# A transformer layer on one core: attention outputs turned by DMA instead of TensorE, and the projection's LayerNorm folded into the residual sum

## The reference, cut to what matters

```python
x = x + _layernorm(attn(_layernorm(x)), eps=1e-5)      # over the last axis, no gain, no shift
x = x + _layernorm(ffn(_layernorm(x)), eps=1e-5)
# attn: qkv = x @ w_attn + b_attn; 16 heads of 32; rope by head index; causal softmax, times E**-0.5;
#       o @ w_proj + b_proj
# ffn:  h = gelu(bitlinear(x, w_fc)); bitlinear(h, w_proj)
# bitlinear(x, w): layer_norm(x, eps=1e-6), absmax-quantised, times ternarised w
```

## Time and profile before

| | |
|---|---|
| median of 3 runs | 1260.82 us (1259.26 to 1261.31) |
| the profiled execution's own time | 1258.53 us |
| its span in the trace | 1256.8 us |
| TensorE busy | 1156.8 us, 92% |
| VectorE busy | 972.4 us, 77% |
| ScalarE busy | 770.1 us, 61% |
| GpSimd busy | 592.8 us, 47% |
| mean granted TensorE clock | 0.977 of full speed |

### The profile page before, as it was taken

How to read it: one execution, slowest core, us unless ns; L and a number is a source line. 1 busy time by engine, 2 the same in 40 slices (tenths; PEclk the granted TensorE clock), 3 DMA queues, 4 the chain that set the end, 5 groups by cost and what they waited for, 6 DMA issues and landing times.

```text
span 1256.8 us, 24649 instructions
## 1 busy us (share of the span) xinstructions
PE 1156.8 (92%) x9204; PEld 634.7 (51%) x9204; DVE 972.4 (77%) x2862; ACT 770.1 (61%) x1430; POOL 592.8 (47%) x658
## 2 busy tenths in 40 slices
PE   6968799999999999999999999999999999987997
PEld 4434444555445554555445554555545554554443
DVE  5988778688787878779796888779786887868634
ACT  5568747675566646675476655766466755577480
POOL 2143216941398125961279314971369412981260
PEclk9978899999999999999999999999999999997999
DMA  9441220123111230121310231112301221001000
GB/s 347 106 159 38 73 59 9 27 60 95 49 36 27 66 112 4 33 60 35 109 25 17 68 89 43 35 33 62 110 5 31 61 80 30 3 2 45 16 9 34
DMA packets 75514, 72.37 MB, mean 58 GB/s; under 512 B 34721, under 2 KB 60289, under 8 KB 74243
## 3 DMA queue, kind: packets, MB, share of 16 engines
q1 hardware_dynamic: 75395, 70.79, 20.1%
HBM read 29.63 MB, written 8.39 MB: 30 GB/s over the span
## 4 chain that ended last, share of the span: by engine, by line
PE 51%; DVE 30%; ACT 11%; issue 3%; POOL 3%; DMA 2%; SPq 1%; POOLq 0%; ACTq 0%; DVEq 0%
PE gen L511 17%; PE down L559 16%; DVE score L1229 8%; PE pv L626 5%; DVE hT L1106 4%; PE score L587 4%; DVE probs L1106 2%; PE gen L578 2%; ACT probs L918 1%; POOL rstd L1620 1%; DVE qkn L1336 1%; DVE bn L1260 1%; DVE mx L1229 1%; DMA x2T<-b_proj 1%; DVE gen L1229 1%
## 5 line engine op out<-in xcount | busy, mean ns | idle before, releaser
L1620 POOL TENSOR_TENSOR rstd<-veps,mhalf 128x1 f32<-128x1 f32 (+1 forms) x104 | 67.0, 644 | 460.5 <-DVE veps L1309 312.4
L918 ACT ACTIVATE probs<-score 128x512 f16<-128x512 f32 x360 | 189.8, 527 | 102.4 <-PE score L602 102.4
L511 PE MATMUL gen<-x2T,t1T 128*128 128x512 f16 x1024 | 240.1, 379 | 3.3 <-ACT x2T L838 1.8
L1106 DVE TENSOR_TENSOR probs<-score,probs 128x512 f16<-128x512 f32 x360 | 199.5, 595 | 45.1 <-ACT score L920 44.0
L559 PE MATMUL down<-t2T,hT 128*128 128x512 f16 x960 | 221.1, 382 | 0.0
L920 ACT ACTIVATE score<-score 128x512 f32<-128x512 f32 x360 | 192.5, 535 | 0.0
L511 PE MATMUL gen<-xT,wa 128*128 128x512 f16 x672 | 156.0, 382 | 4.2 <-DVE mx L1229 3.7
L1106 DVE TENSOR_TENSOR hT<-gen,hT 128x512 f16<-128x512 f32 x156 | 105.8, 685 | 68.6 <-ACT gen L866 34.5
L511 PEld LDWEIGHTS gen<-x2T,t1T 128*128 128x128 f16 x1024 | 95.5, 97 | 107.3 <-ACT x2T L838 4.5
L1229 DVE CUSTOM_DVE_ANT_0 score<-score,mask_rows 128x512 f32<-128x512 f32 (+3 forms) x312 | 143.0, 520 | 0.0
L559 PEld LDWEIGHTS down<-t2T,hT 128*128 128x128 f16 x960 | 90.3, 98 | 98.5 <-issue 2.7
(11 more groups left out here) (190 smaller groups left out, 1822.7 us busy)
## 6 DMA issues: line engine op xcount, KB each, us to landing
qk<-qkn SPq DMA_DIRECT2D x360, 64.0 KB, 2.0
xo<-x SPq DMA_DIRECT2D x8, 1024.0 KB, 5.7
out<-xn SPq DMA_DIRECT2D x31, 256.0 KB, 2.2
hT<-x SPq DMA_DIRECT2D x7, 1024.0 KB, 6.3
hT<-w_fc SPq DMA_DIRECT2D x4, 1024.0 KB, 16.2
hT<-w_down SPq DMA_DIRECT2D x4, 1024.0 KB, 5.2
t2T<-w_qk SPq DMA_DIRECT2D x4, 512.0 KB, 7.4
probs<-w_v SPq DMA_DIRECT2D x1, 1024.0 KB, 10.3
```

The costliest lines, as they stand in the source:

```text
L511: mm = nc.tensor.matmul(bank[:, :], a, b, start=(start and n == 0), stop=(stop and n == len(pairs) - 1))
L918: nc.scalar.activation(probs[:, h % 2, HI, 512 * i:512 * i + n], bank[:, 0:n], ACT.Exp, scale=1.0 / S_UP)
L1106: return V.tensor_tensor(out, whole, hi, ALU.subtract)
```

## The change

The attention outputs of four heads (a chunk of 128 features, `o_chunk[c]`) are split into fp16 halves when the four heads are done, after heads 4, 8 and 12 (`OUT_AT`) and after head 15: `outputs_high` on ScalarE, `outputs_low` on VectorE. SP turns each half with a DMA transpose (`turn_outputs`) straight into the place of `x2T`, one after each `stack(g)`; the last chunk's stand between the first two and the last two heads of `stack(3)`. The fp32 transposes on TensorE and their evictions go. `project` is cut by chunks: `project(0)` and `project(1)` for chunks 0 to 2, then `values(1)`, then the rest. `load_x` waits for the DMA transposes instead of for `o_turn(3)`.

`normalise_y` goes. `first_sum` multiplies the projection's rows in PSUM by `rstd` and adds x in one scalar_tensor_tensor; the row's constant is left out there, where the next LayerNorm takes it away again, and GpSimd adds it to the final LayerNorm's `shift` (`late_shift` keeps one that would be overwritten). `v_low(1)` moves ahead of `y_moments(0)`, `values(1)` on ScalarE ahead of `normalise2(0)`.

```diff
+OUT_AT = {4: 0, 8: 1, 12: 2}
...
-        for name, n in (("v", 0), ("oT", 0), ("oT", 1), ("oT", 2), ("oT", 3), ("v", 1), ("x2T", 0), ("v", 2), ("x2T", 1), ("v", 3),
-                        ("x2T", 2), ("x2T", 3)):
+        for name, n in (("v", 0), ("v", 1), ("x2T", 0), ("v", 2), ("x2T", 1), ("v", 3), ("x2T", 2), ("x2T", 3)):
...
+        oT = x2T
+        o_more = o_more_sb[:, :]
+        o_chunk = [xo[:, c, :].rearrange("p (b e) -> p b e", b=TB) for c in range(EC)]
+        o_rows = [(o_more if c == 0 else xo[:, c - 1, :]).bitcast(f16).rearrange("p (a n) -> p a n", a=2) for c in range(EC)]
...
                     if b != 1:
-                        sp.wait_ge(g_full, g0 - AFTER_O)
+                        for c in range(EC):
+                            sp.wait_ge(oT_in[c], 32 * j)
...
+                def turn_outputs(c):
+
+                    for half in (HI, LO):
+                        sp.wait_ge((o_hi, o_lo)[half], EC * j + c + 1)
+                        sp.dma_start_transpose(oT[:, half, c, :].rearrange("p (b t) -> p b t", b=TB), o_rows[c][:, half, :]
+                                               ).then_inc(oT_in[c], 16)
+
...
@@ -435,7 +448,11 @@
                         row = TB * j if isinstance(j, int) else sp.snap(TB * j)
                         sp.dma_start(xres, x_v[:, bass.ds(row, TB), :]).then_inc(xres_in, 16)
                     if nxt:
-                        stack(g)
+                        stack(g, range(2) if g == 3 and here else range(4))
+                    if here:
+                        turn_outputs(g)
+                    if nxt and g == 3 and here:
+                        stack(g, range(2, 4))
                     if prev:
                         for tb in ((), (0, 1), (2,), (3,))[g]:
                             store(tb)
...
-
-                    if tb == 0:
-                        pe.wait_ge(o_scaled, len(SCALED))
-                        pe.wait_ge(o_ready, HEADS * (j + 1) - len(SCALED))
-                    bank = claim("oT", tb)
-                    turn(bank, lambda c: xo[:, tb, PARTS * c:PARTS * (c + 1)]).then_inc(g_full, 1)
-
-                def project(tb):
-
-                    if setup and tb == 0:
-                        pe.wait_ge(w_ready, 2)
-                    if tb < 3:
-                        pe.wait_ge(s_drained, s0 + S["scores", HEADS - 1 if nxt else HEADS - 2] + tb + 1)
-                    else:
-                        pe.wait_ge(pv_drained, HEADS * (j + 1))
+                def project(tb, c0, c1):
+
                     bank = y_banks[tb]
-                    products(bank, [(lift[:, :], p_bias[:, :])], stop=False)
-                    pe.wait_ge(oT_hi, TB * j + tb + 1)
-                    products(bank, [(oT[:, tb % 2, HI, c, :], wp[:, b, c, :]) for c in range(EC) for b in (HI, LO)],
-                             start=False, stop=False)
-                    drained("oT", tb)
-                    products(bank, [(oT[:, tb % 2, LO, c, :], wp[:, HI, c, :]) for c in range(EC)], start=False
-                             ).then_inc(y_full, 1)
+                    if c0 == 0:
+                        if setup and tb == 0:
+                            pe.wait_ge(w_ready, 2)
+                        if tb < 3:
+                            pe.wait_ge(s_drained, s0 + S["scores", HEADS - 1 if nxt else HEADS - 2] + tb + 1)
+                        else:
+                            pe.wait_ge(pv_drained, HEADS * (j + 1))
+                        products(bank, [(lift[:, :], p_bias[:, :])], stop=False)
+                    rows = slice(PARTS * tb, PARTS * (tb + 1))
+                    for c in range(c0, c1):
+                        pe.wait_ge(oT_in[c], 32 * (j + 1))
+                        last_one = products(bank, [(oT[:, HI, c, rows], wp[:, HI, c, :]), (oT[:, HI, c, rows], wp[:, LO, c, :]),
+                                                   (oT[:, LO, c, rows], wp[:, HI, c, :])], start=False, stop=(c == EC - 1))
+                    if c1 == EC:
+                        last_one.then_inc(y_full, 1)
 
                 def x2_turn(tb):
...
                 if here:
-                    o_turn(0)
-                    o_turn(1)
-                    project(0)
-                    o_turn(2)
-                    project(1)
-                    o_turn(3)
-                    project(2)
-                    project(3)
+                    project(0, 0, EC - 1)
+                    project(1, 0, EC - 1)
+                    if nxt:
+                        values(1)
+                    project(0, EC - 1, EC)
+                    project(1, EC - 1, EC)
+                    project(2, 0, EC)
+                    project(3, 0, EC)
                     if setup:
                         pe.wait_ge(tern_ready, 2 * FC)
                         for u in range(FC):
                             mm = nc.tensor.matmul(down[:, :], ones16[:, :], t2T[:, u, :], start=(u == 0),
                                                   stop=(u == FC - 1))
                         mm.then_inc(c_full, 1)
-                    if nxt:
-                        values(1)
...
-                    nc.scalar.activation(y_sb[:, tb % 2, :], y_banks[tb][:, :], ACT.Identity,
-                                         bias=shift[:, LP, tb:tb + 1], scale=rstd[:, LP, tb:tb + 1]
-                                         ).then_inc(y_ready, 1)
+                def outputs_high(c):
+
+                    done = 4 * (c + 1)
+                    need(act, o_scaled, len([h for h in SCALED if h < done or not setup]))
+                    act.wait_ge(o_ready, HEADS * j + done - len([h for h in SCALED if h < done or not setup]))
+                    need(act, o_lo, EC * j + c)
+                    high(o_rows[c][:, HI, :], o_chunk[c].rearrange("p b e -> p (b e)")).then_inc(o_hi, 1)
 
                 def normalise2(tb):
                     if tb < 2 and prev:
...
+                    if here and h in OUT_AT:
+                        outputs_high(OUT_AT[h])
...
                         final(FINISH_AT[h])
                 if here:
+                    outputs_high(EC - 1)
                     if nxt:
                         values(0)
-                    o_turned(0)
-                    o_turned(1)
-                    o_turned(2)
                     if prev and nxt:
                         final(3)
-                    normalise_y(0)
-                    o_turned(3)
-                    normalise_y(1)
-                    normalise2(0)
-                    normalise_y(2)
-                    normalise2(1)
-                    normalise_y(3)
                     if nxt:
                         values(1)
+                    normalise2(0)
+                    normalise2(1)
                     x2_turned(0)
                     if nxt:
                         values(2)
...
-                    V.tensor_tensor(xo[:, :, HD * h:HD * (h + 1)], oA[:, h % 2, :, :],
+                    V.tensor_tensor(o_chunk[h // 4][:, :, HD * (h % 4):HD * (h % 4 + 1)], oA[:, h % 2, :, :],
                                     r_sum[:, h % 2, :].unsqueeze(2).to_broadcast([PARTS, TB, HD]), ALU.mult
...
-                    low(oT[:, tb % 2, LO, :, :], blocks(bank_of("oT", tb)), oT[:, tb % 2, HI, :, :]
-                        ).then_inc(g_drained, 1)
+                def outputs_low(c):
+
+                    dve.wait_ge(o_hi, EC * j + c + 1)
+                    low(o_rows[c][:, LO, :], o_chunk[c].rearrange("p b e -> p (b e)"), o_rows[c][:, HI, :]).then_inc(o_lo, 1)
 
                 def y_moments(tb):
 
...
-                    dve.wait_ge(y_ready, n + 1)
-                    V.tensor_tensor(x1_out[:, tb, :], y_sb[:, tb % 2, :], xres[:, tb, :], ALU.add).then_inc(x1_ready, 1)
+                    dve.wait_ge(ln_ready[LP], n + 1)
+
+
+                    V.scalar_tensor_tensor(out=x1_out[:, tb, :], in0=y_banks[tb][:, :], scalar=rstd[:, LP, tb:tb + 1],
+                                           in1=xres[:, tb, :], op0=ALU.mult, op1=ALU.add).then_inc(x1_ready, 1)
...
                         head_output(h)
+                        if h in OUT_AT:
+                            outputs_low(OUT_AT[h])
...
                 if here:
+                    outputs_low(EC - 1)
                     if nxt:
                         v_low(0)
-                    o_low(0)
-                    o_low(1)
                     if prev and nxt:
                         final(3)
                         final_moments(3)
                         final_terms(3)
+                    if nxt:
+                        v_low(1)
                     y_moments(0)
-                    o_low(2)
                     y_moments(1)
-                    o_low(3)
                     first_sum(0)
                     y_moments(2)
                     first_sum(1)
                     y_moments(3)
                     first_sum(2)
-                    if nxt:
-                        v_low(1)
                     x2_low(0)
                     first_sum(3)
...
```

(20 more changed lines are left out.)

28 lines of the change are left out of this document (8 added, 20 removed).

## The result

| | before | after |
|---|---|---|
| median | 1260.89 us (1259.26 to 1261.31) | 1243.53 us (1239.58 to 1248.29) |
| after / before | | 0.9865, 95% interval 0.9833 to 0.9897 |
| profiled execution, its span | 1258.53, 1256.8 us | 1239.58, 1237.9 us |
| TensorE, VectorE busy | 1156.8, 972.4 us | 1139.9, 968.9 us |
| ScalarE, GpSimd busy | 770.1, 592.8 us | 746.7, 595.9 us |

A forecast was written before the change was run, and what follows sets the result against it. The usual tail was taken as bound by VectorE's LayerNorm chain, close to TensorE. Six usual batches 12.0, set-up 2.8, last batch 2.4, less 0.3 at the end, give 16.9 us saved: 1243.9 us, range 1239 to 1252.5.

The forecast's parts named there:

- 2.0 us a usual batch: Tail of each of six usual batches: VectorE's last small operation starts at 477.3 instead of 479.28, 12.0 us in all.
- the end's 0.3: At the kernel's very end, GpSimd's added small operation in the final LayerNorm is paid once, 0.27 us.
- rival C: Usual tail: TensorE is the bound, the sums cost no more; 2.5 us a batch, 1241 us; chance 0.15.
- `v_low(1)` leaving the chain with its wait (1.37): VectorE's usual tail: v_low(1) and its wait on ScalarE leave the chain, 0.6 + 0.77 us saved.
- a first sum 0.8 earlier: VectorE's usual tail: first_sum(0) starts at 466.8 instead of 467.62, 0.8 us earlier.
- 0.24 for dearer sums: VectorE's usual tail: the four first sums, now reading PSUM with a factor, cost 0.24 us more together.
- Part 2: Normalisation moved into first_sum: each sum with moments 1.91 us for 1.85, four times; GpSimd's addition 0.27 us.
- Covered: Head loop: subtractions at heads 4, 8, 12 cost nothing, hidden by VectorE's waits; 1.8 us a batch if uncovered.
- the 2.8 that this batch was to bring: Set-up batch's tail: VectorE waits there, so TensorE's whole saving counts, 2.8 us.
- The 0.6: Last batch with heads, before the tail: VectorE is the bound, so the subtraction at head 12 costs 0.6 us.
- A: Head loop gives the gain back: VectorE passes 1.8 us a batch to TensorE, 1256.5; chance 0.15 from 1249 up.
- B: Tail: last chunk's DMA transposes land late, about 10 us slower, 1271; chance 0.07 slower, 0.05 about break-even.

The follow-up runs named there:

- repeat: The changed kernel run once more with nothing edited; 1242.85 us, ratio 0.9871 to the kernel before.
- negm_once: Changed kernel with the four per-block negated means of y taken out of VectorE's chain, one for all behind first_sum(3); 1239.99 us, ratio 0.9852.
- more_products: Changed kernel with eight more TensorE products in the tail, four each in project(2) and project(3); 1249.05 us, ratio 0.9916.
- turn_only: Changed kernel with normalise_y kept on ScalarE: outputs turned by DMA, values(1) and v_low(1) still moved forward; 1252.26 us, ratio 0.9941.
- fold_only: Kernel before with only the normalisation folded into first_sum and GpSimd's extra addition, outputs still turned by TensorE; 1248.76 us, ratio 0.9919.
- best: Changed kernel, set-up chunks handled at heads 7, 9, 12, one negated mean for all blocks, values(1) back behind project(3) in usual batches; 1236.37 us, again 1238.13.
- late_chunk: Changed kernel with the last chunk's two transposes behind all twelve DMAs of stack(3) instead of behind six; 1249.02 us, ratio 0.9918.
- values_late: Changed kernel with values(1) back behind project(3), its eviction and v_low(1) also back in their old places; 1243.27 us, ratio 0.9867.
- best_2: As best, with the set-up batch's first three chunks handled at heads 10, 11 and 13, transposes behind stack(2); 1235.61 us, ratio 0.9806.

## Why the prediction was right, and where it was not

- The number and the size per batch. 2.0 us a usual batch was 2.07, the end's 0.3 was 0.32, the head loop of a usual batch cost nothing, the landings took 2.5 us in the median (2.4 to 4.1) and were hidden. In the usual tail the steps came where they were forecast, counted from `weigh(15)`'s start: moments at 9.0 us (9.0), the first sum at 11.3 (11.25), the last small operation at 21.8 (21.7). The last operation of the chain was forecast 19.9 us after `weigh(15)`'s end in the last batch and came 1165.71 - 1145.8 = 19.9 after it. That the median of after lies 0.4 us from the forecast is in part luck: its four times span 8.7 us, and between spans the saving was 18.9 us with the first profile and 14.6 with that of repeat, for 16.9 forecast. In the first profile two misses cancel, +2.2 in the set-up heads and 2.35 less than forecast in the loop of the last batch.
- VectorE's chain as the bound, against rival C. Right in the usual batches by negm_once and more_products; the set-up tail is TensorE's, also as forecast, 3.24 for 2.8.
- Which part earns it. The sum was made of `v_low(1)` leaving the chain with its wait (1.37) and a first sum 0.8 earlier, less 0.24 for dearer sums. As places in VectorE's queue the three held: the wait and `v_low(1)` are gone, the first sum starts 0.86 earlier (12.11 to 11.25 us after `weigh(15)`), each sum costs 0.06 more. Which edit brings them was taken wrongly. The wait of 0.77 goes by the fold alone, since ScalarE has four steps less; `v_low(1)` moved forward with values(1) ahead of the last chunk's products holds the chain's start back by 1.9 us, more than it saves, and hides 0.76 of what the turning gives. Part 2 was costed only by its dearer sum; that ScalarE's step between power and sum stood in the chain (1.2 us at the first sum) was not in it as a saving, and my expectations of turn_only and fold_only repeated that mistake after the result.
- The set-up batch. "Covered" was read from waits of a usual batch and taken for all. Its VectorE was not read in the set-up heads. A wait of 1.57 us more at head 4 is uncovered there, more than half of the 2.8 that this batch was to bring. That GpSimd can hold such a subtraction was in the text, with the price of 0.9 from the division; it took 0.84 more, at the place where no slot was free. The rest of the 2.0 to 4.5 us by which the set-up heads are longer in the kernels with the early chunk stays open: the clock dips there in every kernel, at other heads in each, and no run separates these dips from the change.
- The last batch. The tail was right (3.0 for 3.25). The loop gained 1.75 instead of losing 0.6, in a stretch that took 96.4 to 101.1 us across the kernels of the table; and 96.37 or 100.62 for one and the same kernel (best); so that gain says nothing about the change. In the two first profiles the same 825 instructions keep TensorE busy for 85.39 us at a granted clock of 0.93 before and for 82.28 at 0.96 after, more than the whole 1.75. The 0.6 is neither confirmed nor refuted.
- Rivals A and B. A did not happen in the usual batches and has its point in the set-up one. B is a matter of 1.8 us of slack (2.1 forecast), as late_chunk showed, and did not decide in after. C did not happen as told: the sums did cost 0.24 more, and TensorE is not the bound of a usual batch in after; it is near: behind the landing its waits add up to 0.7 us in values_late (0.43 and 0.26) and to 0.26 in best. The Trainium skill's price for a 128x128 transpose through DMA ("VectorE: DVE Perf Modes", "The three transpose paths") does not describe this: each half of a chunk, four blocks, lands in 2.5 us, and with 1309 ns a block (an estimate from that page's figure: eight blocks from 454.23 on, 464.7) TensorE would have waited in after at 459.31, which it does not.

## What to carry to other kernels

A step on another engine in the middle of a chain costs its hand-over where the chain has no other work to do meanwhile, here at the first of four sums. So a fold that makes the consumer dearer by 0.06 us was worth more (1.69 us a batch) than taking 2.8 us of work and waiting off another engine (1.14 on top of it); price it by the start of the first dependent instruction, not by its own duration. "It is hidden" has to be read in each kind of batch, set-up too. When a change is cut into halves to see which earns, a third edit that rides in one of them has to be cut out too. A piece of work used as cover for a transfer should not be longer than the transfer needs: here it hid the DMA and held back the chain.

## What the hardware showed

VectorE's 16-bit in-place pass over 128x512 in SBUF took 293 ns at heads 8 and 12, and 1134 to 1247 ns at head 4 while GpSimd worked on SBUF. The subtraction with two SBUF inputs took 1.52 us in the set-up batch, where it started inside a product of GpSimd, and 0.68 in the set-up batch of best_2, where it comes after GpSimd's last product. In the usual batches of after it meets GpSimd too, and there GpSimd pays. In all six the two start within 0.01 us of each other, and GpSimd's sum L1654 takes 1.80 us instead of 1.26 (in before none of these sums takes more than 1.28):

```profile
402.50 0.68 DVE L1104 TENSOR_TENSOR o_more<-xo,o_more 128x512 f16<-128x512 f32 x1
402.51 1.80 POOL L1654 TENSOR_TENSOR acc<-acc,acc_add 128x512 f32<-128x512 f32 x1
```

So which of the two is held changes with who comes first; that this is the rule is read from these cases, not tested. The Trainium skill ("GPSIMD Engine Reference", "1. Specifications") names contention for SBUF interfaces with VectorE for two kinds of instruction (two SBUF inputs, or a 2-port perf mode); the trace agrees for the first, by a factor of 2. The in-place pass is slower by a factor of 4; that it runs in such a mode no row here tells.

SP's issue of the last chunk's two 128x512 transposes took 2.52 us in the first usual batches and up to 3.48 in later ones of the same run (values_late, its last usual batch). It is hidden in after, and it is what varies in values_late and best. In late_chunk the two take 2.55 to 2.60 throughout, and it is their start that slips, from 4.96 to 5.80 us after `weigh(15)`. Why SP is slower there is open.
